# Attention stepped by rounds of value products, with eight products with Wo inside the last head

## What is computed

```python
h = _layernorm(x) * (1 + ca) + sa                      # x: 4 batches, 2048 tokens, 512 channels
q, k, v = split(h @ Wqkv.T + bqkv); q, k = rope(q), rope(k)   # 16 heads of 32
att = softmax(where(causal, q @ k.T / sqrt(32), -inf))
x = x + ga * ((att @ v) @ Wo.T + bo)
h = _layernorm(x) * (1 + cb) + sb
x = x + gb * experts(h)                                # top 8 of 48 kept experts, gates from a softmax
```

## Time and profile before

| | us |
|---|---|
| median of 3 executions | 4518.87 (4517.97 to 4528.74) |
| the profiled execution | 4511.35 |
| its span | 4509.5 |
| busy: PE, DVE, ACT, POOL | 3907.1, 2760.9, 1819.8, 2777.2 |
| batch 0: first score, last head, first product with Wo | 260.6, 851.0, 920.58 |

### The profile page before, as it was taken

One profiled execution on the slowest core, in us unless ns is written; L12 is line 12 of the kernel. 1 busy time (PEld: TensorE's weight loads), 2 busy tenths in 40 slices (PEclk: granted clock), 3 DMA queues, 4 the chain that ended last, 5 costly groups with the idle time before them and its releaser, 6 DMA issues.

```text
span 4509.5 us, 85283 instructions
## 1 busy us (share of the span) xinstructions
PE 3907.1 (87%) x21344; PEld 2270.5 (50%) x21344; DVE 2760.9 (61%) x5837; ACT 1819.8 (40%) x3526; POOL 2777.2 (62%) x2251
## 2 busy tenths in 40 slices
PE   2989999876989999687899999669899999659998
PEld 1754444345744444256644444357544444347776
DVE  2767677445757767365667766366666775446665
ACT  1335555522345555332355555223355555211111
POOL 2757788723768778615678878407677877305554
PEclk7989999987989999898999999889999999879999
DMA  5443333242533333333433332424423332439997
GB/s 188 157 137 83 89 94 99 52 166 99 176 105 94 77 94 100 111 108 133 160 85 95 89 91 75 148 97 152 138 76 93 86 97 63 169 102 246 257 257 194
DMA packets 305622, 555.81 MB, mean 123 GB/s; under 512 B 59892, under 2 KB 99956, under 8 KB 301812
## 3 DMA queue, kind: packets, MB, share of 16 engines
q1 hardware_dynamic: 283640, 491.91, 36.1%
q0 software_dynamic: 21504, 58.40, 5.5%
HBM read 318.15 MB, written 174.85 MB: 109 GB/s over the span
## 4 chain that ended last, share of the span: by engine, by line
PE 54%; issue 16%; POOL 13%; SPq 5%; DMA 5%; DVE 4%; ACT 2%; POOLq 1%; DVEq 0%; ACTq 0%
PE PS L1232 13%; PE PS L1184 11%; PE PS L1208 8%; PE PS L1338 6%; PE PS L1262 5%; POOL Sm L925 4%; PE PS L1349 4%; POOL qs L898 3%; POOL t L895 3%; SPq L664 3%; DMA QK<-mT 2%; SPq L697 2%; POOL hTl L873 2%; PE PS L1275 2%; PE PS L1211 1%
## 5 line engine op out<-in xcount | busy, mean ns | idle before, releaser
L1046 ACT ACTIVATE Pt<-PS 128x512 f32<-128x512 f32 (+3 forms) x2560 | 1226.7, 535 | 1138.6 <-PE PS L1208 664.7
L1481 DVE TENSOR_REDUCE part<-PS 128x1 f32<-128x512 f32 x1536 | 1018.0, 686 | 706.6 <-PE PS L1184 704.5
L925 POOL TENSOR_TENSOR Sm<-Pt 128x512 f32<-128x512 f32 (+3 forms) x960 | 1029.5, 1076 | 480.1 <-ACT Pt L1046 356.6
L1184 PE MATMUL PS<-QK 96*128 96x512 f32 (+3 forms) x2560 | 920.5, 423 | 114.8 <-DVE part L1481 47.6
L1232 PE MATMUL PS<-Pt,V 128*32 128x512 f32 (+3 forms) x5120 | 949.7, 554 | 62.4 <-POOL Sm L925 62.3
L1236 PE MATMUL PS<-Sm,onesv 128*32 128x512 f32 (+3 forms) x1920 | 865.4, 533 | 0.0
L1208 PE MATMUL PS<-QK 97*128 97x512 f32 (+3 forms) x2560 | 818.7, 392 | 39.7 <-DMA QK<-mT 31.6
L1184 PEld LDWEIGHTS PS<-QK 96*128 96x128 f32 x2560 | 418.2, 191 | 821.0 <-DVE part L1481 355.5
L925 POOL TENSOR_TENSOR Sm<-Sm,Pt 128x512 f32<-128x512 f32 (+1 forms) x640 | 711.8, 1112 | 50.2
L1477 DVE CUSTOM_DVE_ANT_0 PS<-PS,consts 128x128 f32<-128x128 f32 (+3 forms) x1024 | 499.7, 494 | 105.8 <-PE PS L1184 102.3
L1208 PEld LDWEIGHTS PS<-QK 97*128 97x128 f32 x2560 | 486.7, 195 | 150.8 <-issue 54.0
(11 more groups left out here) (165 smaller groups left out, 4705.1 us busy)
## 6 DMA issues: line engine op xcount, KB each, us to landing
QK<-qkd SPq DMA_DIRECT2D x720, 128.0 KB, 3.1
qkd<-st SPq DMA_DIRECT2D x64, 1024.0 KB, 4.5
Wg<-wgu SPq DMA_DIRECT2D x48, 768.0 KB, 4.8
o<-od SPq DMA_DIRECT2D x448, 64.0 KB, 2.0
W<-wd SPq DMA_DIRECT2D x4, 6144.0 KB, 17.5
Wd<-wdn SPq DMA_DIRECT2D x48, 384.0 KB, 5.8
xin<-x SPq DMA_DIRECT2D x16, 1024.0 KB, 7.5
vd<-vst SPq DMA_DIRECT2D x16, 1024.0 KB, 6.1
```

The source lines that it names most:

```text
L925: nc.gpsimd.tensor_tensor(total, of[0][:, first:CH] if i == 1 else total, of[i][:, first:CH], ALU.add).then_inc(sum_done, 1)
L1046: nc.scalar.activation(Pt[:, t % NPT, first:CH], S2[t % NS2][:, first:CH], ACT.Exp, scale=SCALE).then_inc(exp_done, 1)
L1184: mm(s1[:, 0:w], QK[0:3 * HD, hh % 2, 0, qb * P:(qb + 1) * P], QK[0:3 * HD, hh % 2, 1, c * CH:c * CH + w], start=True, stop=True).then_inc ...
L1481: v.reduce_max(part[:, qb, cc:cc + 1], s1[:, 0:w], AX.X).then_inc(s1_dve, 1)
```

## The change

Attention is stepped by rounds in place of units: 15 steps a head, each with the scores of a round's two or three tiles, the value of the round three steps back, its `plus`, and about three `max`. There are four sums Sm. `negated` stands directly behind the first `max` that follows its `row`. The `max` of head 1 begin at step 4, those of the others at step 2, and both end at step 0 of the next head. Joins, reciprocals (two a step) and scales of a group stand 3 to 5 steps behind the copy.

In the last head, chunk by chunk, the output is joined and scaled at once, and eight products with Wo (chunks 0 and 1) stand at the steps of `OUT_AT`, with their residuals and statistics; the norm of chunk 0 follows. SP loads `otc` and `xc` of these chunks in head 13, and POOL widens them in head 14. Behind the meeting stand the last join, reciprocals and scale, beside the turns and logits of chunk 0. SP sends a row of maxima before the moves of the last chunk, and loads W only when the last scale is done. The functions `widen`, `join`, `scale`, `spread_of`, `norm`, `rows_out`, `residual`, `moments`, `shift` and `inverse` are the code of before, moved so that both stages can call them. The cores of the diff:

```diff
-    tiles = [(qb, c, min(CH, (qb + 1) * P - c * CH)) for qb in range(NT) for c in range(qb // TPC + 1)]
-    units = [(j, kb) for j in range(NCH) for kb in range(0, TPC * (j + 1), 2)]
-    return tiles, units
-TILES, UNITS = plan()
-NTILE, NU = len(TILES), len(UNITS)
-ENDS = [max(u for u in range(NU) if UNITS[u][0] == j) for j in range(NCH)]
+    return [(qb, c, min(CH, (qb + 1) * P - c * CH)) for qb in range(NT) for c in range(qb // TPC + 1)]
+TILES = plan()
+NTILE = len(TILES)
 SHAPES = ((2, 2), (3, 2, 3), (3, 3, 3, 3), (3, 3, 3, 3, 2, 2))
 ROUNDS = [(j, tuple(range(sum(shape[:r]), sum(shape[:r + 1])))) for j, shape in enumerate(SHAPES) for r in range(len(shape))]
 NR = len(ROUNDS)
-NPT, NSM, LAG = 12, 3, 3
+NPT, NSM, LAG = 12, 4, 3
...
+FIRST_TILES_FROM = 4
+OUT_AT = (8, 9, 10, 11, 12, 13, 14, 16)
 def stream():
-    closing = [[] for _ in range(NU * H + 16)]
-    beside = [[] for _ in range(NU * H)]
+    closing = [[] for _ in range(NR * H + 12)]
+    beside = [[] for _ in range(NR * H)]
+    negated = {}
     for i in range(LAST_CHUNK, NTILE):
         beside[(i - LAST_CHUNK) // 4].append(("max", 0, i))
     beside[2].append(("most", 0, 1))
     beside[3] += [("row", 0, 1), ("negated", 0, 1)]
     for hh in range(1, H):
-        at = NU * (hh - 1) + TILES_FROM
+        late = TILES_FROM if hh > 1 else FIRST_TILES_FROM
+        at, span = NR * (hh - 1) + late, NR + 1 - late
         for i in range(NTILE):
-            beside[at + i * NU // NTILE].append(("max", hh, i))
+            beside[at + i * span // NTILE].append(("max", hh, i))
             if i in (FIRST_HALF - 1, NTILE - 1):
-                half, n = int(i >= FIRST_HALF), at + i * NU // NTILE
+                half, n = int(i >= FIRST_HALF), at + i * span // NTILE
                 beside[n + 1].append(("most", hh, half))
                 beside[n + 2].insert(0, ("row", hh, half))
-                closing[n + 2].append(("negated", hh, half))
-    ends = {NU * hh + ENDS[j]: (hh, j) for hh in range(H) for j in range(NCH)}
-    for n, (hh, j) in ends.items():
-        closing[n + LAG].append(("copy", hh, j))
-        if hh % GH == GH - 1:
-            closing[n + 7].append(("join", hh // GH, j))
-            for i in range(TPC):
-                closing[n + 7 + i].append(("inverse", hh // GH, j, i))
-            closing[n + 7 + TPC].append(("scale", hh // GH, j))
-    due = [[] for _ in range(NU * H + 16)]
+                negated[n + 2] = ("negated", hh, half)
+    for n, step in negated.items():
+        beside[n].insert(2, step)
     for hh in range(H):
-        for r in range(NR):
-            due[NU * hh + DUE[r]].append(("value", hh, r))
-            beside[min(NU * hh + DUE[r] - LAG, NU * H - 1)].append(("plus", hh, r))
-    closing[NU * (H - 3)].append(("fold",))
-    closing[NU * H + 2].append(("widen", 0))
-    closing[NU * H + 6].append(("widen", 1))
+        for j in range(NCH):
+            n = NR * hh + LAST_ROUND[j] + LAG
+            closing[n].append(("copy", hh, j))
+            if hh == H - 1 and j < NCH - 1:
+                closing[n + 2] += [("join", NG - 1, j), *(("inverse", NG - 1, j, i) for i in range(TPC))]
+                closing[n + 3].append(("scale", NG - 1, j))
+            elif hh % GH == GH - 1 and hh < H - 1:
+                closing[n + 3].append(("join", hh // GH, j))
+                for i in range(TPC):
+                    closing[n + 3 + i // 2].append(("inverse", hh // GH, j, i))
+                closing[n + 5].append(("scale", hh // GH, j))
+    last = NR * (H - 1)
+    for i, t in enumerate(OUT_AT):
+        closing[last + t].append(("out", *divmod(i, TPC)))
+        if i == TPC - 1:
+            closing[last + t].append(("moments",))
+    closing[last + NR].append(("normed",))
+    closing[NR * (H - 3)].append(("fold",))
+    closing[NR * (H - 2) + 1].append(("widen", 0))
+    closing[NR * (H - 2) + 7].append(("widen", 1))
     out = []
-    for n in range(NU * H + 16):
-        if n < NU * H:
-            out.append(("score", *divmod(n, NU)))
-        out += due[n]
-        if n < NU * H:
-            out += beside[n]
+    for n in range(NR * H + 12):
+        if n < NR * H:
+            out.append(("score", *divmod(n, NR)))
+        if LAG <= n < NR * H + LAG:
+            out.append(("value", *divmod(n - LAG, NR)))
+        if n < NR * H:
+            out += [("plus", *divmod(n, NR))] + beside[n]
         out += closing[n]
     return out
-NV, NPT_B = NR * H, 2 * NU * H
+NV, NPT_B = NR * H, NTILE * H
...
-    out = [("out", 0, t) for t in range(TPC)] + [("stat", 0), ("norm", 0)]
+    out = [("join", NG - 1, NCH - 1)]
     for j in range(NCH):
         more = j + 1 < NCH
-        if more:
+        if j and more:
             out += [("out", j + 1, 0), ("out", j + 1, 1)]
         out += [("turn", j, ct) for ct in range(KT)] + [("logit", j)]
         if j:
             out.append(("slot", j - 1))
+        else:
+            out += [("inverse", NG - 1, NCH - 1, i) for i in range(TPC)] + [("scale", NG - 1, NCH - 1), ("widen", 2)]
         out.append(("gate", j))
+        if j and more:
+            out += [("out", j + 1, 2), ("out", j + 1, 3)]
         if more:
-            out += [("out", j + 1, 2), ("out", j + 1, 3), ("stat", j + 1)]
+            out.append(("stat", j + 1))
+        if j == 0:
+            out.append(("widen", 3))
         out += [("back", j, t) for t in range(TPC)] + [("old", j, 0), ("old", j, 1), ("new", j)]
...
+                    max_row(hh - 1, 1)
                     if hh >= 2:
                         move(hh - 2, NCH - 1)
-                    max_row(hh - 1, 1)
...
+                    if hh == H - 2:
+                        for j in range(2):
+                            load_attention(j)
+                            load_tokens(j)
...
+                store_tokens(0)
+                load_attention(2)
+                load_tokens(2)
                 move(H - 1, NCH - 1)
...
+                store_tokens(1)
+                load_attention(3)
+                load_tokens(3)
+                wait_apart(sp, ot_ready[NCH - 1], NG * (b + 1))
                 sp.dma_start(W[:, :, :, :, :].bitcast(F32), wd).then_inc(w_in, 16)
...
+                def widen(j):
+                    if j < 2:
+                        pool.wait_ge(gabo, ONE + b + 1)
+                        pool.wait_ge(c_in[j % 2], ONE + 32 * b + 16)
+                    else:
+                        pool.wait_ge(c_in[j % 2], ONE + 32 * (b + 1))
+                    nc.gpsimd.tensor_tensor(xc[:, j % 2], xc[:, j % 2], rows[:, 1:2].broadcast_to([P, TPC, C]), ALU.add).then_inc(xg_ready, 1)
...
+                        if j == 0:
+                            act.wait_ge(ot_ready[NCH - 1], ONE + NG * (b + 1))
...
+                def rows_out(j, t):
+                    if j == 0 and t == 0:
+                        pe.wait_ge(wo_gated, ONE + KT * (b + 1))
+                        pe.wait_ge(mt_ready, ONE + N_ROW * (b + 1))
+                    if t == 0:
+                        pe.wait_ge(y_in[j % 2], ONE + 48 * (2 * b + j // 2 + 1))
+                        pe.wait_ge(ot_ready[j], ONE + NG * (b + 1))
+                    pe.wait_ge(y_used, ONE + TPC * NCH * b + max(TPC * j + t - 1, 0))
+                    for k in range(KT):
+                        rows_of = otc[:, j % 2, k, t * P:(t + 1) * P] if k < NG - 1 else ot[:, j * CH + t * P:j * CH + (t + 1) * P]
+                        last = mm(PS[:, t % 2], rows_of, wot[:, k, :], start=k == 0, stop=k == KT - 1)
+                    last.then_inc(y_ps, 1)
...
+                def residual(j, t):
+                    ci = NCH * b + j
+                    if j == 0 and t == 0:
+                        dve.wait_ge(s2_ready, ONE + NPT_B * b + NTILE * (H - 1))
+                    if t == 0:
+                        dve.wait_ge(xg_ready, ONE + ci + 1)
+                        dve.wait_ge(x1_out[j % 2], ONE + 32 * b + 16 * (j // 2))
...
+                    elif kind == "moments":
+                        moments(0)
+                        shift(0)
```

195 lines of the change are left out of this document (95 added, 100 removed).

## The result

The changed kernel takes 4466.2 us (median of four executions, 4457.5 to 4467.4), the kernel before 4522.5 us (4518.0 to 4528.7) on the same chip. The ratio is 0.987, with an interval of 0.985 to 0.989. The profiled execution took 4467.4 us around a span of 4465.6, 43.9 us less than the span before; the sum said 45.6.

What follows compares the result with a forecast made beforehand. PE was taken to bound fourteen heads of attention, with long standing at each batch's end. Per batch -22.7 - 3.1 + 14.4 (heads) = -11.4 us, -46 us in four: 4473 us as a median, range 4360 to 4525.

Steps and rivals of the forecast that it cites:

- The last head: End of each batch: from the last head's start to the first turn 70.5 us against 93.2, -22.7 us a batch.
- the 5 us fall away: End of batch: 3 us behind the meeting and 2 us behind the 5.2 us wait, added for the slower clock; without them 4453.
- Third maximum waits: In the heads: the third maximum waits for its bank's negation, 1.0 us in one half, 0.85 in the other; +26 us a batch.
- the first rival: In the heads: the third maximum hardly waits, giving back 104 us, time 4370; chance 20%.
- Short units, 0.4 us a head: In the heads: units without a value round, two maxima 1.1 us after two others, vanish; -5.6 us a batch.
- Group ends +3 us: Heads at the end of a group: a pair of them costs 4.5 us of waits instead of 3.5; +3 us a batch.
- 0 within 2 us: Head 0: head 1's later first maximum waits less for its operand, but twelve rounds hold forty maxima; no net change.
- Chunk 0's -3.1 us: Behind the first turn: two products no longer stand between logits and turns back, so the next step starts earlier; -3.1 us a batch.
- The slower one: In the heads: the maxima of every round wait, now in threes on three banks; at 0.1 us a round 4551; chance 17%.
- the last one: Last head: the change doesn't fill it, value rounds behind products still wait for POOL; head 69.5 us, time 4505; chance 8%.
- no change to be told: Meeting and last head as priced, group ends at 5.6 us, head 0 slower by 2, first product 3 us later; 4507; 15%.
- middle heads under 37 us: Sign that the forecast is wrong and the third maximum hardly waits for the row's negation; middle heads were expected near 38.1 us.

Runs made afterwards that it cites:

- e4: Changed kernel with the eight products with Wo behind the last head's last value products, joins still inside the head: 4461 us, last head to first turn 70.8 us.
- e4b: Changed kernel with the eight products with Wo and the last group's joins, reciprocals and scales (chunks 0 to 2) behind the last value products: 4436 us, stretch 64.2 us.
- e8: Changed kernel with products and joins behind the last value products, and loads and widenings of chunks 0 and 1 back behind the last move: 4465 us, stretch 85.8 us.
- e2: Changed kernel with the turn of a row of maxima and its negation ahead of the round's value products, not behind them: 4338 us.
- e3: Changed kernel with the reciprocals at a group's end one a round over four rounds, not two a round over two: 4392 us.
- e7: Changed kernel with the loads for chunks 0 and 1 issued in the first third of head 13, not at its end: 4426 us.
- e5: Changed kernel with head 0's second row of maxima sent behind the first three of head 1's twelve operand loads, not behind all twelve: 4433 us.

## Why the prediction was right, and where it was not

**The number came out by errors that cancel.** Point by point:

- The last head was priced well in most of its parts: PE's first stretch 15.8 us (15.6 said), the first product 21.5 us after the head's start (20.8), a wait of 5.5 us (5.2), 3.84 us in the meeting (4), the turn after 69.4 us in batch 0 and 68.4 in the mean (70.5). Two slips in the sum hide behind that. Its terms give 54.7 + 5.2 = 59.9 us for the head and not 61.5. And the 3 us for the clock behind the meeting can't delay the turn that ends this stretch; they belong behind it, and there they came (see chunk 0). Without both, the forecast is 59.9 + 2 + 4 = 65.9 us: the head's own work, done at 927.6, which is 65.5 us after its start, was 3.6 us dearer than priced. Further, the text sought the gain in products that fill the last head. e4 and e4b show that this placing costs 4 us, and e8 that the gain is mostly a load: in the earlier trace rows the widening at 907.30 had waited 11.56 us for the tokens, and the 25.36 us of PE stood behind it. The row was read, and its consequence was not drawn.
- The stands cost clock as the rows at 1030 said. The first product took 5.46 us for six matmuls against 2.84 in the next ones, the logits 5.88 against 3.84. From the Trainium skill, "TensorE: Matmul & The Clock Gate", What's actually happening, the prediction took that the slow clock is the default and that activity releases it. That short stands would therefore be cheap and the 5 us fall away was its own conclusion, and it did not come true: with both stands the granted clock went to 1.2 GHz, from 882.7 to 889.5 and from 930.5 to 940.7.
- "Third maximum waits": right in place and mechanism, a little too dear, 1.4 us a middle head against 1.85. This was the dispute with the first rival (20%), and e2 settles it: with row and negation ahead of the value products the time is 4338. The rival's 4370 was on the right side, but half of e2's gain lies in heads 4, 8 and 12, which it had not priced.
- "Short units, 0.4 us a head" is the term that was mis-sized most for the middle heads. Head 6 without any wait is 34.6 us, and the sum for it was 37.3 - 0.5 - 0.4 = 36.4. Of the 1.8 us too many, 0.4 are waits (PE stood 0.92 us in that head, not 0.5) and 1.4 busy time (1.8 us saved, not 0.4), most of it for maxima, 14.25 us before and 11.7 in e2. The trace shows part of why: in a run of maxima the second starts 0.335 us after the first, the third 0.231 after the second, and before there were twenty runs of two a head, now fourteen, nearly all of three. That makes 0.6 us; how the rest divides between the dearer runs without a value round, such as 0.97 us for the two at 516.32 in head 6 of the kernel before, and late banks was not separated.
- "Group ends +3 us": too low. Heads 3, 7 and 11 gained 2.5 us each, but heads 4, 8 and 12 lost 4.7. Over two middle heads such a pair cost 2.5 us before (3.5 said) and 8.0 after (4.5 said). The count of DVE's time was made without the negation: a pair of reciprocals ahead of it lengthens the wait that was priced at 1.0 us, and the slow clock comes on top. e3 shows both.
- Missing altogether: the moved loads as a load on the DMA engines. The prediction asked only POOL's queue for slack for the widenings, and there it was right. Head 14 got 11.4 us longer, and e7 takes 12.2 off it.
- Head 0, "0 within 2 us": +2.8. The change took away the 7.6 us for head 1's operands, which the text named but did not size, and made PE wait 4.9 us for the row behind SP's twelve issues; e5 without that wait is 2.9 us below the kernel before. What used up the rest of the gain no run shows. The reading of the waits that found two names over 1 us a batch had left out this one, 30.3 us in four waits of the same view as the earlier trace rows.
- Chunk 0's -3.1 us did not show: from the turn to the next batch it got 4.0 us longer, 2.7 of them before the turn of chunk 1. The traces show that the clock took it back. In e8, where the granted clock is 1.00 from the first turn of batch 0 up to 945.1, the step that was at 961.34 comes 14.1 us after this turn, against 17.2 before the change, which is the 3.1. In the changed kernel it comes after 17.1 us (16.5 in the mean), because the logits of 5.88 us lie in a slow stretch (930.5 to 940.7). A second one, from 947.6 to 957.8, makes what follows longer; before the change the same 26.3 us had a granted clock of 1.00. It begins within the second of two stands of 2.50 and 1.75 us, where the kernel before had PE at work on the two products that were moved away. W is loaded as late in e8 as in the changed kernel, and e8 is only 0.9 us longer than the kernel before from turn to next batch, so the late load alone does not explain the 4.0.

The changed kernel in these 26.3 us (columns as in the earlier trace rows):

```profile
931.50:957.80 26.30, 19.31 (x102) 15.76 (x103) 14.27 (x40) 8.97 (x14) 13.80 (x6) 0.63 0.97 375
```

**The rivals.** The slower one (maxima of all rounds wait) did not happen: in e2's head 6 PE does not stand at all with three maxima a round. Nor did the last one: a value round behind a product waited for nobody, PE was at work for 44.1 of the 48.0 us behind the wait, and 3.84 of the rest are the meeting. Of the third, "no change to be told", two parts came, head 0 slower and the group ends dearer; the middle heads made up for them.

**The marks.** The text called middle heads under 37 us a sign that the row is cheap. They are 36.4 (36.5 in the mean), and it was not: a mark on a sum of two unknown terms cannot tell which of them was off. The waits by name could, and did.

## What to carry to other kernels

- Ask of a long stand behind a join or a meeting what its last engine itself was waiting for. Here it was a load that could be issued two heads earlier; moving the work of the bounding engine about brought less than nothing.
- In a ring of few buffers, the use with the long way back (PE to DVE to PE) should stand ahead of a block of other work and its answer right behind it. Two steps moved in the list gave 129 us, more than twice what the whole change gave.
- A transfer that is moved needs a look at what is sent right behind it, in bytes, and not only at the queue of the engine that uses it.

## What the runs showed of the hardware

- A stand of PE of 1.84 us, with small ones before it, was followed by the lower clock (0.51 granted) for 6.9 us of full work; in the same head of the third batch it was not. The waits of 0.56 and 0.85 us in the middle heads of the changed kernel never were. Which stands are followed by it could not be told from the traces. What it cost beside the stand was 3.1 us in head 4 (42.1 against 39.0) and 5.7 in head 12 (47.8 with 20.5 us at the low clock, 42.1 in the last batch with 6.8).
- Two products less between the logits and the gates of chunk 0 are worth 3.1 us at a granted clock of 1.00 (e8), and nothing at the same step in the changed kernel, where 10.2 us of this stretch were at the low clock.
- The same 41 maxima of a head took 14.25, 12.21 and 11.74 us of PE by their order alone, at a granted clock of 1.00.
- A load of 128 KB that lands after 3.0 to 3.6 us took 9.8 us behind 3.5 MB of others.
